# Attention batches of a fused transformer block: maxima spread between other VectorE work, routing last, normalisations on Pool

## The reference, cut to what matters

```
x = x + 0.5 * moe(layernorm(x))
x = x + attention(layernorm(x))
x = x + 0.5 * moe(layernorm(x))

moe(x):  logits = x @ Wg + bg; top 2 of 8 experts, softmax over the two
         y_e = gelu(x @ W1[e] + b1[e]) @ W2[e] + b2[e]
         return layer_norm(x + sum of the two y_e by their shares) * gamma + beta
attention(x):  16 heads of width 8; q, k, v = x @ w.T; rotary positions on q and k
         softmax(q k^T / sqrt(8)) v, then @ w_o.T
```

## Time and profile before

| | us |
|---|---|
| median of 3 runs | 492.79 (488.77 to 493.09) |
| the profiled execution | 494.3 |
| its span | 492.5 |
| PE busy | 405.1 (82%) |
| DVE busy | 355.2 (72%) |
| ACT busy | 256.0 (52%) |
| POOL busy | 213.9 (43%) |

### The profile page before, as it was taken

One profiled execution on the slowest core, in us unless ns is written; L12 is line 12 of the kernel. 1 busy time (PEld: TensorE's weight loads), 2 busy tenths in 40 slices (PEclk: granted clock), 3 DMA queues, 4 the chain that ended last, 5 costly groups with the idle time before them and its releaser, 6 DMA issues. The chain is left out here.

```text
span 492.5 us, 10357 instructions
## 1 busy us (share of the span) xinstructions
PE 405.1 (82%) x3224; PEld 331.3 (67%) x3224; DVE 355.2 (72%) x1148; ACT 256.0 (52%) x515; POOL 213.9 (43%) x268
## 2 busy tenths in 40 slices
PE   1542599999999986989988989899998999999910
PEld 1442388898798864666656666676587888888800
DVE  4798335646776858999999999886465755568856
ACT  2520256765556444666665746575565456555500
POOL 5488764583544311212113243424046658335531
PEclk9999999999999998899999999999799999999965
DMA  9612812123111015980000000001112121132331
GB/s 283 250 38 56 247 38 55 55 55 92 44 44 32 24 55 201 310 265 23 1 23 13 12 13 13 23 12 34 45 32 60 46 66 49 49 98 68 89 107 43
DMA packets 32691, 37.71 MB, mean 77 GB/s; under 512 B 4992, under 2 KB 27520, under 8 KB 32240
## 3 DMA queue, kind: packets, MB, share of 16 engines
q1 hardware_dynamic: 27632, 27.32, 18.7%
q0 software_dynamic: 4544, 9.35, 5.8%
q10 hardware_dynamic: 464, 0.38, 0.3%
HBM read 26.64 MB, written 20.36 MB: 95 GB/s over the span
## 5 line engine op out<-in xcount | busy, mean ns | idle before, releaser
L1187 ACT ACTIVATE stage<-ps 128x512 f32<-128x512 f32 x78 | 46.7, 598 | 81.1 <-PE ps L722 80.8
L1768 DVE TENSOR_REDUCE mx<-ps 128x4 f32<-128x1024 f32 x64 | 77.3, 1214 | 8.9 <-PE ps L835 8.8
L1654 DVE TENSOR_TENSOR ring_hi<-ps,ring_hi 128x512 fp32r<-128x512 f32 x78 | 53.9, 691 | 36.7 <-ACT ring_hi L1194 36.2
L1241 ACT ACTIVATE stage<-ps 128x1024 f32<-128x1024 f32 x64 | 65.5, 1023 | 26.7 <-PE ps L846 25.9
L745 PE MATMUL ps<-w_hl,ring_hi 128*128 x234 | 65.5, 348 | 0.9 <-DVE stage L1662 0.9
L499 POOL DMA_INDIRECT expert_y<-stage x39 | 38.9, 998 | 53.4 <-DVE stage L1662 52.7
L746 PE MATMUL ps<-w_hl,ring_hi 128*128 x312 | 61.1, 237 | 0.0
L480 POOL DMA_INDIRECT sorted_x<-rows,place_at x32 | 35.6, 1112 | 54.8 <-DVE place_at L1475 48.3
L1648 DVE TENSOR_TENSOR bx<-ps,bx 128x128 fp32r<-128x128 f32 x78 | 22.5, 288 | 50.1 <-ACT bx L1169 49.6
L499 POOL DMA_INDIRECT expert_y<-stage,arena x39 | 38.9, 996 | 42.9 <-DVE stage L1662 38.3
L746 PEld LDWEIGHTS ps<-w_hl,ring_hi 128*128 128x128 f32 x312 | 54.6, 193 | 0.0
(11 more groups left out here) (197 smaller groups left out, 1056.5 us busy)
## 6 DMA issues: line engine op xcount, KB each, us to landing
sorted_x<-fill SPq DMA_DIRECT2D x8, 1096.5 KB, 16.9
stage<-w SPq DMA_DIRECT2D x16, 256.0 KB, 6.7
y_got<-expert_y SPq DMA_DIRECT2D x24, 128.0 KB, 2.3
stage<-sorted_x SPq DMA_DIRECT2D x39, 64.5 KB, 1.8
arena<-sorted_x SPq DMA_DIRECT2D x39, 64.5 KB, 1.8
x_tok<-x SPq DMA_DIRECT2D x4, 256.0 KB, 4.9
sorted_x<-rows,place_at POOLq DMA_INDIRECT x64, 2.4
stage<-sel SPq DMA_DIRECT2D x1, 1024.0 KB
```

Source lines behind the costliest of these rows:

```text
L1187: act.activation(g_full[:, s, :], ps[:, H_BANK, :], ACT.Gelu).then_inc(g_done, 1)
L1241: act.activation(prob[:, 2 * v:2 * v + 2, :], ps[:, at:at + 2, :], ACT.Exp, scale=SCALE)\
L1654: vec.tensor_tensor(bg_lo[:, s, :, :].rearrange("p c n -> p (c n)"), ps[:, G_BANK, :], bg_hi[:, s, :, :].rearrange("p c n -> p (c n)").bit ...
L1768: vec.tensor_reduce(mx[:, t, :].rearrange("p (r g j) -> p r j g", r=2, g=2)[:, pair, 2 * jp:2 * jp + 2, :], ps[:, at:at + 2, :].rearrange( ...
```

## The change

On VectorE, in batches 1 to 5: the first part of `combine` (and of the sums) goes behind maximum 0, the second part behind the second `divide`, the statistics for attention ahead of maximum 4, and `gating` with `add_chosen` behind maximum 7. Batch 0 keeps its order, but takes maxima 0 and 1 together with `combine(2)` as before. The rotation's sum is written by VectorE straight into the rounded tile, and Pool computes the unrounded sum itself before it subtracts. Both normalisations leave VectorE for Pool (`att_apply`, `pre_apply`), except for unit 11, which the second list still normalises on VectorE. In Pool's own list the rsqrt steps and `att_apply` come before the scatters, and `pre_apply` between the two scatters of a batch. In `gating` the subtraction for the shares goes to the end. TensorE gets two filler matmuls ahead of `qk_swapped` in batches 1 to 5. In the second list, TensorE computes the totals and last ranks at the end of slot 7, and VectorE does `rank_blocks` ahead of `placing`.

```diff
@@ -455,6 +455,22 @@
                 gp.tensor_tensor(prstd[:, i % 2, :], prstd[:, i % 2, :], neg_half[:, 0:BT], ALU.pow)\
                     .then_inc(post_rstd, 1)
 
+            def att_apply(b):
+                gp.wait_ge(att_norm[2], 2 * b + 2)
+                gp.wait_ge(a_xt_filled, b)
+                for t in range(BT):
+                    op = gp.tensor_scalar(xn[:, t, :], x_tok[:, b * BT + t, :], mv[:, t, 0:1], rstd[:, t:t + 1],
+                                          ALU.subtract, ALU.mult)
+                op.then_inc(a_ln_done, 1)
+
+            def pre_apply(u):
+                first, many = unit_tiles(u)
+                gp.wait_ge(rstd_ready, 2 * u + 2)
+                for c in range(first, first + many):
+                    op = gp.tensor_scalar(rows1[:, c, 0:D], x_tok[:, c, :], fmv[:, c, 0:1], frstd[:, c:c + 1],
+                                          ALU.subtract, ALU.mult)
+                op.then_inc(ln_done, 1)
+
             def gate_exp(phase):
                 gp.wait_ge(gap_ready, FIRST_UNIT if phase == 0 else UNITS)
                 gp.tensor_tensor(e2[:, :], euler[:, :], gap[:, :], ALU.pow).then_inc(e2_ready, 1)
@@ -490,6 +506,11 @@
                                  bet.unsqueeze(1).broadcast_to([P, GT, D]), ALU.add).then_inc(beta_added, 1)
 
             def low_rotated(b, p):
+                gp.wait_ge(sin_done, b + 1)
+                if b:
+                    gp.wait_ge(rot_ready, b)
+                gp.tensor_tensor(rot, t_cos, t_sin, ALU.add).then_inc(rot_sum, 1)
+                gp.wait_ge(rot_sum, b + 1)
                 gp.wait_ge(rot_hi_done, b + 1)
                 gp.tensor_tensor(rot_lo[:, p, :, :], rot, rot_hi[:, p, :, :].bitcast(F32),
                                  ALU.subtract).then_inc(rot_ready, 1)
@@ -544,17 +565,24 @@
 
                 if b >= 2:
                     second_ids(PAIRS + b - 2)
+                if b >= 1 and norm:
+                    post_rstd_of(b + 3)
+                    att_rstd(b + 3)
+                    att_apply(b + 3)
                 if b == BATCH - 1:
                     scatter(PAIRS + b - 3, 0, 1)
-                elif b >= 3:
-                    scatter(PAIRS + b - 3, 0)
                 if b >= 1:
                     pre_rstd(FIRST_UNIT + b - 1)
                 if more:
                     low_rotated(b + 2, p)
-                if norm:
+                if 3 <= b < BATCH - 1:
+                    scatter(PAIRS + b - 3, 0)
+                if b >= 1:
+                    pre_apply(FIRST_UNIT + b - 1)
+                if b == 0:
                     post_rstd_of(b + 3)
                     att_rstd(b + 3)
+                    att_apply(b + 3)
                 if 3 <= b < BATCH - 1:
                     scatter(PAIRS + b - 3, 1)
 
@@ -1006,6 +1034,9 @@
                     qk(b + 2, p)
                 step(b, p, 5, place_next)
                 if project_next:
+                    if b:
+                        scores_owned(b + 1, 6)
+                        keep_busy(2 * (6 % MAX_BUF), 2)
                     qk_swapped(b + 2, p)
                 if tail and not last:
                     pe.wait_ge(att_done, b + 1)
@@ -1088,6 +1119,9 @@
                     transpose_y(b, M1)
                 if s == 4:
                     rank(u - 1)
+                if s == 7:
+                    totals(3)
+                    rank(u)
 
             def amid_second(s):
                 b = BATCH - 1
@@ -1098,9 +1132,6 @@
                     transpose_x(u)
                 if s == 6:
                     router(u)
-                if s == 7:
-                    totals(3)
-                    rank(u)
 
             def attention():
                 pe.wait_ge(y_done, SLOTS)
@@ -1427,8 +1458,6 @@
                     op = vec.max(top[:, t, :], logits[:, t, :])
                 op.then_inc(gate_steps, at.up())
                 vec.wait_ge(gate_steps, at.now())
-                vec.tensor_tensor(gap[:, first:first + many], top[:, 0:many, 1], top[:, 0:many, 0], ALU.subtract)\
-                    .then_inc(gap_ready, 1)
                 for t in range(many):
                     op = vec.max_index(top_at[:, t, :], top[:, t, :], logits[:, t, :])
                 op.then_inc(gate_steps, at.up())
@@ -1442,6 +1471,8 @@
                 vec.wait_ge(gate_steps, at.now())
                 vec.tensor_tensor(members[:, u % 2, FRONT:FRONT + many, :], picks[:, u % 2, 0, 0:many, :],
                                   picks[:, u % 2, 1, 0:many, :], ALU.add).then_inc(members_set, 1)
+                vec.tensor_tensor(gap[:, first:first + many], top[:, 0:many, 1], top[:, 0:many, 0], ALU.subtract)\
+                    .then_inc(gap_ready, 1)
 
             def add_chosen(u):
 
@@ -1745,6 +1776,9 @@
 
             def rotate_cos(b, bank=M1):
                 vec.wait_ge(qk_filled, b + 1)
+                if b:
+                    vec.wait_ge(rot_sum, b)
+                    vec.wait_ge(rot_hi_done, b)
                 vec.tensor_tensor(t_cos, ps[:, bank, :].rearrange("p (m n) -> p m n", m=2),
                                   rope_sb[:, 0:1, :].broadcast_to([P, 2, SEQ]), ALU.mult).then_inc(cos_done, 1)
 
@@ -1754,11 +1788,7 @@
                 vec.tensor_tensor(t_sin, ps[:, bank, :].rearrange("p (m n) -> p m n", m=2),
                                   rope_sb[:, 1:2, :].broadcast_to([P, 2, SEQ]), ALU.mult).then_inc(sin_done, 1)
                 vec.wait_ge(sin_done, b + 1)
-                if not (isinstance(b, int) and b == 0):
-                    vec.wait_ge(rot_ready, b)
-                vec.tensor_tensor(rot, t_cos, t_sin, ALU.add).then_inc(rot_sum, 1)
-                vec.wait_ge(rot_sum, b + 1)
-                vec.tensor_copy(rot_hi[:, p, :, :], rot).then_inc(rot_hi_done, 1)
+                vec.tensor_tensor(rot_hi[:, p, :, :], t_cos, t_sin, ALU.add).then_inc(rot_hi_done, 1)
 
             def maxima(b, *us):
                 for u in us:
@@ -1798,12 +1828,17 @@
                                   x_tok[:, tiles(b, BT), :], ALU.add).then_inc(att_done, 1)
 
             def batch(b, p, tail=True, place_next=True, project_next=True, norm=True):
+                u = FIRST_UNIT + b - 2
+                late = 1 <= b < BATCH - 2
                 if place_next:
                     maxima(b + 1, 0)
-                if place_next:
+                if b == 0:
                     maxima(b + 1, 1)
-                if b == 0:
                     combine(2, apply_part=False)
+                if late and norm:
+                    combine(b + 3, apply_part=False)
+                if b and place_next:
+                    maxima(b + 1, 1)
                 if tail:
                     divide(b - 1, 0)
                 if b == 0:
@@ -1816,6 +1851,8 @@
                     a_norm(2, stats_part=False)
                 if tail:
                     divide(b - 1, 1)
+                if late and norm:
+                    combine(b + 3, sum_part=False)
                 if not place_next:
                     list_blocks(2)
                 if place_next:
@@ -1827,12 +1864,15 @@
                     low_y(b - 1)
                 if b >= 3 and place_next:
                     placing(FIRST_UNIT + b - 3)
+                if late and norm:
+                    vec.wait_ge(x_done, b + 4)
+                    a_norm(b + 3, apply_part=False)
                 if place_next:
                     maxima(b + 1, 4)
                 if tail:
                     add_attention(b - 1, M0 if place_next else Y_BANK)
                 if b >= 2:
-                    logits_of(FIRST_UNIT + b - 2)
+                    logits_of(u)
                 if tail:
                     vec.wait_ge(att_done, b + 1)
                     pre_stats(FIRST_UNIT + b - 1)
@@ -1842,24 +1882,23 @@
                     maxima(b + 1, 5)
                 if project_next:
                     rotate_sin(b + 2, p)
-                if b >= 2:
-                    gating(FIRST_UNIT + b - 2)
-                    add_chosen(FIRST_UNIT + b - 2)
-                if norm:
+                if b == 0:
                     combine(b + 3, apply_part=False)
+                if b >= 2 and not late:
+                    gating(u)
+                    add_chosen(u)
                 if place_next:
                     maxima(b + 1, 6)
-                if norm:
+                if b == 0:
                     combine(b + 3, sum_part=False)
                     vec.wait_ge(x_done, b + 4)
                     a_norm(b + 3, apply_part=False)
                 if place_next:
                     maxima(b + 1, 7)
                     negate(b + 1, 1)
-                if norm:
-                    a_norm(b + 3, stats_part=False)
-                if tail:
-                    pre_apply(FIRST_UNIT + b - 1)
+                if b >= 2 and late:
+                    gating(u)
+                    add_chosen(u)
                 if b == BATCH - 2:
                     placing(FIRST_UNIT + 4)
                     rank_blocks(2)
```

(2 more changed lines are left out.)

## The result

The changed kernel took 495.57 us (median of 20 runs, 494.04 to 497.81), the kernel before 492.55 on the same chip (20 runs, 488.46 to 496.42): a ratio of 1.0064, with a 95% interval of 1.0048 to 1.0080. Slower by 0.6%, which is within the 1% of the middle case; 494.7 was forecast. Ratios and their intervals leave out executions of over 1.5% above the fastest of the same kernel; the medians given beside them do not. The profiled execution took 494.2 (span 492.4), 0.1 less than that of before (span 492.5). Per step the traces must therefore be compared with each other, and 3 us of the medians' difference are not in them. The longer runs of after are those with a lower mean granted clock: 494.0 to 494.5 us go with 0.962 to 0.964, 497.5 and more with 0.953.

What follows compares the result with a forecast made beforehand. VectorE sets attention's pace, TensorE within about 10%, and work ahead of the cosine product matters. 494.3 + 1.3 (attention) + 1.5 (clock) - 0.9 (second list) = 496.2, or 494.7 on the median's scale; range 489 to 502.

Steps and rivals of the forecast that it cites:

- the middle case: Whole kernel: the time stays within about 1% (4.9 us) of the kernel before; chance 0.57.
- The path through the cosine product: Batches 1 to 4: the path through TensorE makes the 2.1 us removed from VectorE nearly vanish; -1.45 us together.
- the port: Attention: VectorE stalled beside Pool's SBUF operations, +0.6 us each in batches 3 and 4, 0 in batch 0.
- The first rival: Attention and list: VectorE stays the bound, each microsecond taken off returns; 483.0 us, 481.5 on the median's scale; chance 0.12.
- The clock: Batch 1: TensorE waits for the low part of y, one fall of the granted clock, +1.5 us, bounds 0 and 3.5.
- The second rival: Batches 1 to 4: clock falls in each at the cosine product wait, 1.5 to 2.5 us each; 502.7 us; chance 0.25.
- The lead of TensorE: Start of batch 5: TensorE's lead on VectorE's first maximum falls from 4.3 to 1.7 us, a further delay of 2.6.
- Moved, and what it now delays: Batches 1 to 4: sums and application ahead of the cosine product, gating behind the last maximum; batch 4 23.0 against 23.21 us.
- The second list: Second list: wait and low clock at the totals go, 2.7 us, less 1.8 at block 13's load; gain 0.9.
- the one for placing behind the block ranks: Second list: placing stands behind twelve chained block-rank instructions of about 0.16 us, so 1.9 us.

Runs made afterwards that it cites:

- the best version: Kernel before with normalisations on Pool; in batches 1 to 5 sum between maxima 6 and 7, gating, application and statistics behind 7; 506.33 us, ratio 0.9899.
- the offload run: Kernel before with both normalisations on Pool, gap's subtraction last, second list's part, order of maxima kept; 511.14 us, ratio 0.9913; again 508.25, 0.9976.

## Why the prediction was right, point by point

**The path through the cosine product: right.** For batch 4 it said 14.0 + 5.94 + 3.06 = 23.0 without the port; the trace says 13.67 + 5.84 + 3.21 = 22.72. VectorE's idle time ahead of the last maximum, forecast at 1.5 to 2, is 2.21. Batch 2: 22.4 forecast, 22.14 measured. The first rival (VectorE stays the bound) is refuted by that idle time, and batch 5 of the run with the work behind maximum 7 shows that it comes from the missing cover behind the cosine product, as the prediction said. The rival's price was also not quite right: the copy that goes was given none (it took 0.43 at 198.81 in the kernel before), and batch 1 has no gating whose stall could go.

**The clock: right in place and size.** One fall, in batch 1, behind the wait for the low part of y. Forecast 1.5, measured 2.0 by the run with fillers. The wait is 1.77, not over 2: it follows a wait of 1.03 for a maximum, which I had not put ahead of it. Batch 1 took 23.70; the forecast gives 21.9 + 1.5 = 23.4. The second rival's falls in batches 3 and 4 did not come in any trace of the changed kernel; they came when the normalisations were left on VectorE, and once in batch 3 of the best version, behind a wait of 0.78 for the cosine product. So that rival was near.

**The lead of TensorE: right in mechanism, too small.** From TensorE's first step of batch 5 to VectorE's first maximum there are 0.97 us (297.53 to 298.50) where I had 1.7: the lead lost is 3.35, not 2.6. Batch 5 from step to step is 21.69 (forecast 21.3) against 22.41.

**The port: wrong place.** I charged 0.6 in batches 3 and 4 for Pool's normalisations beside the gating. They do stand beside it, and block nothing: the gating behind the last maximum took 1.72 (274.06 to 275.78) against 1.76 without a stall. VectorE's two comparisons, with two inputs in SBUF, and Pool's two normalisations there:

```profile
274.94 0.26 DVE L1468 TENSOR_TENSOR picks<-const,top_f 128x16 f32<-128x16 f32 x2
```

```profile
274.30 1.62 POOL L470 TENSOR_SCALAR rows<-x_tok,fmv,frstd 128x128 f32<-128x128 f32 x2
```

The comparisons take the 0.26 that they take alone. I took 0 in batch 0, and there the stall was 2.1 us, 1.1 more than before. Its length shows no loss all the same. It came out 1.25 shorter than in the profile of before, but that is chance and not the change: the run with the list's part alone has the attention of before and a batch 0 of 25.51, and the changed kernel itself took 26.99 in another trace. It goes in part with how long the clock is low in this batch. The kernel before is at 0.57 from 192 to 200, the changed kernel is through with it sooner:

```profile
188.00:192.00 4.00, 2.93 (x8) 2.23 (x8) 2.90 (x10) 1.01 (x1) 1.60 (x4) 0.68 0.12 35
192.00:196.00 4.00, 2.80 (x26) 1.58 (x24) 3.92 (x8) 1.42 (x3) 0.11 (x1) 0.89 1.09 381
196.00:200.00 4.00, 3.45 (x46) 2.74 (x50) 3.96 (x6) 2.52 (x3) 1.87 (x2) 1.00 1.11 335
```

In the other two traces it is the other way round, 0.57 over 4 us in the list's part alone (196 to 200), 0.67 and 0.50 over 8 us in the changed kernel (200 to 208). With a short fall batch 0 took 25.51 before and 25.61 after, with a long one 26.86 and 26.99 (though 25.63 in a third trace of the changed kernel): like with like, the change costs batch 0 about 0.1.

The rule quoted in the prediction from the Trainium skill (SBUF — State Buffer, "Who interferes with whom") agrees with the double stall: two of Pool's instructions with two inputs, two blocked sums. For Pool's normalisations the trace does not bear it out: by the rule they would have blocked the comparisons above, which start and end within them as the profile dates them, and the measurement decides. The same section says that a cast can take both ports too, under conditions on its operands; the conversion that took 0.81 instead of 0.17 in the offload run agrees with that, and my reading of it in the prediction, which left one-input forms out, was too narrow.

**Not seen: the wait of the cosine product for Pool's sum** in the first list, +1.29. The step that failed is "Moved, and what it now delays": I looked at the new wait in attention, where none shows, and not in the first list, where Pool's queue holds a scatter that waits 2.5 us for a block result. The run with the rotation alone put back has no such wait; for the size of the term there are the two traces of the first chip (1.29) and the means over all traces (1.4 apart, with the scatter told above).

**The sum at TensorE's first step of batch 6**: +1.3 (first list) - 1.25 (batch 0) - 0.6 (batches 1 to 4, where I had -1.45 + 1.2 + 1.5 = +1.25) + 3.35 (lead) - 0.7 (batch 5) = +2.1, which is 319.22 against 317.11. The forecast there, with its fall, was +2.8. So the total came out near by offsets, which is luck: the 1.3 of the first list was missed, and the -1.25 of batch 0 that cancels it is chance between two traces; the port's 1.2 were not there, the lead's 0.7 were missing.

**The second list: right sign, gain larger.** The wait at the totals fell from 1.62 to 0.16 and the low clock behind it is gone; the wait for block 13's load grew from 0.58 to 1.66, as predicted, with no fall of the clock after it. The delay of +2.1 is +1.8 at the list's first block result and -0.1 at its last (469.53 against 469.63), so the list gave 1.9 where I had 0.9. By VectorE's results of the blocks it gained 2.9 at the totals (before 377.3 to 383.3, after 379.2 to 382.3) and gave 1.1 back at block 13's load; the forecast had 2.7 and 1.8. The mis-sized term is the one for placing behind the block ranks. In runs of that part alone the gain is not to be told from nothing.

**Open.** The profiles differ by -0.1 and the medians by +3.0. With the chance of batch 0 taken out the profiles would differ by about +1.2 (an estimate, -0.1 + 1.25), which accounts for part of the gap. The forecast was +1.9 on either scale. Which falls of the clock make the longer runs of after longer is not shown, since each kernel has one trace on that chip. Why ScalarE stands still on the other chips, and why the loss is 1.6 to 1.9% there, is not shown either. The traces only place a part of it: from batch 6's first maximum to the second list's first block result the changed kernel took 46.4 us on the first chip (47.0 before) and 56.7 and 56.8 on two others, where the run with the list's part alone took 52.3. Of the change itself, the two fillers and Pool's new order were not run apart from VectorE's order.

## What to carry to other kernels

When two engines hand work to each other within a loop, lay out the path from one hand-over to the next for both and move work only to where the other engine is not waiting: here the gating and the sums had filled the time that TensorE needs from the cosine product to the last maximum, and with both moved away, ahead and behind, VectorE idled 2.2 us a batch. With the sums left in that stretch it did not. Work taken off an engine can pay where the order stays (here in one series of two) and won nothing that the runs show under the new order, and a sum moved to Pool can cost more than it saves, by the stalls beside it and by the wait that comes with it; look at each place in the program that calls the moved helper, not only at the loop that the edit is for. Test an offload and a reordering in separate runs: the one gave -0.9% and -0.2% in two series, the other +1.6%. And compare two traces of the same kernel before explaining a difference of 1 us between two kernels.
